# Bias of a top-3 expert layer as one bf16 pass over three-part factors, and a new order of the side work

## The reference

```python
# x: (8, 512, 256)
q, k = rope(x @ Wq.T), rope(x @ Wk.T)            # one head of 256, bf16
o = sum over keys of exp(q k / 16), causal        # one number per token
x = layernorm(x + relu(o * fc1_w + fc1_b) @ fc2_w.T + fc2_b)
xa = x @ P_w.T
C1, C2, C3 = top-3 softmax weights of xa @ U.T over 12 experts, for U1, U2, U3
h = gelu(sum_e C1[:, e] * (x @ W1[e].T))
y = sum_e C2[:, e] * (h @ W2[e].T) + C3 @ b2
out = layernorm(x + y)
```

## Time and profile before

| | us |
|---|---|
| median of 3 runs (323.3 to 323.86) | 323.63 |
| the profiled execution, its own time | 323.53 |
| its span, first to last instruction | 321.8 |
| busy: TensorE / VectorE / ScalarE / POOL | 282.4 / 250.2 / 155.8 / 115.0 |

### The profile page before, as it was taken

One profiled execution on the slowest core, in us unless ns is written; L12 is line 12 of the kernel. 1 busy time (PEld: TensorE's weight loads), 2 busy tenths in 40 slices (PEclk: granted clock), 3 DMA queues, 4 the chain that ended last, 5 costly groups with the idle time before them and its releaser, 6 DMA issues.

```text
span 321.8 us, 6235 instructions
## 1 busy us (share of the span) xinstructions
PE 282.4 (88%) x1976; PEld 191.8 (60%) x1978; DVE 250.2 (78%) x744; ACT 155.8 (48%) x327; POOL 115.0 (36%) x264
## 2 busy tenths in 40 slices
PE   0999999979784989999999999999999997989981
PEld 0444455444333668677677667677678576667770
DVE  0169789999976579689789879888978977887672
ACT  1138747657561381435635634633733753724331
POOL 1000028999999102142332331522333324132221
PEclk9999999999985999999999999999999999999998
DMA  8999999900000000000010001000100010011011
GB/s 232 415 404 229 200 151 211 144 3 0 0 1 0 3 2 0 18 18 18 18 33 17 18 18 29 22 18 18 34 20 16 18 34 19 18 33 26 26 35 37
DMA packets 19235, 20.58 MB, mean 64 GB/s; under 512 B 1600, under 2 KB 18432, under 8 KB 18688
## 3 DMA queue, kind: packets, MB, share of 16 engines
q1 hardware_dynamic: 18480, 19.22, 24.8%
q10 hardware_dynamic: 720, 0.93, 1.0%
HBM read 15.94 MB, written 4.19 MB: 63 GB/s over the span
## 4 chain that ended last, share of the span: by engine, by line
DVE 25%; PE 21%; issue 6%; ACT 5%; POOL 3%; DVEq 0%; POOLq 0%
PE bank L832 17%; DVE early L1202 11%; DVE st L1239 3%; DVE stats L1038 2%; DVE top L1059 2%; ACT x L548 2%; DVE early L1244 2%; PE bank L784 2%; ACT early L657 1%; POOL rstd L391 1%; PE bank L741 1%; DVE mv L1240 1%; ACT x1T L555 1%; ACT early L604 1%; DVE esum L1104 1%
## 5 line engine op out<-in xcount | busy, mean ns | idle before, releaser
L832 PE MATMUL bank<-W,early 128*128 (+1 forms) x630 | 75.5, 273 | 4.4 <-DVE early L1244 2.3
L832 PE MATMUL bank<-W,x1T 128*128 (+1 forms) x630 | 76.9, 277 | 0.5 <-DVE early L1202 0.3
L832 PEld LDWEIGHTS bank<-W,x1T 128*128 128x128 f16 x630 | 60.3, 99 | 19.8 <-DVE early L1202 9.5
L688 PE MATMUL bank<-early,wqk 128*128 128x512 f32 x128 | 64.3, 634 | 8.5 <-DMA gatew<-in_gate 8.5
L1202 DVE SCALAR_TENSOR_TENSOR early<-bank,Csel,early 128x256 f32<-128x256 f32 x124 | 59.3, 479 | 15.0 <-PE bank L832 10.5
L832 PEld LDWEIGHTS bank<-W,early 128*128 128x128 f16 x630 | 60.1, 98 | 14.8 <-DVE early L1244 3.3
L457 POOL TENSOR_SCALAR ve<-mv 128x1 f32<-128x1 f32 x32 | 7.3, 230 | 117.2 <-DVE mv L1240 117.2
L688 PEld LDWEIGHTS bank<-early,wqk 128*128 128x128 f32 x128 | 23.5, 201 | 30.1 <-issue 20.9
L604 ACT ACTIVATE early<-early 128x256 f32<-128x256 f32 x32 | 13.3, 417 | 48.0 <-DVE early L1202 47.9
L499 ACT ACTIVATE qk<-bank 128x512 bf16<-128x512 f32 x32 | 19.0, 594 | 35.6 <-PE bank L688 35.4
L599 ACT ACTIVATE early<-bank,Csel 128x256 f32<-128x256 f32 x31 | 14.6, 472 | 31.0 <-PE bank L832 30.7
(11 more groups left out here) (107 smaller groups left out, 422.3 us busy)
## 6 DMA issues: line engine op xcount, KB each, us to landing
early<-in_xT SPq DMA_DIRECT2D x16, 256.0 KB, 9.8
xs<-in_x SPq DMA_DIRECT2D x32, 128.0 KB, 7.3
out<-early SPq DMA_DIRECT2D x32, 128.0 KB
W<-in_w1T SPq DMA_DIRECT2D x1, 2048.0 KB, 12.0
W<-in_w2T SPq DMA_DIRECT2D x1, 2048.0 KB, 12.3
W<-in_w1T SPq DMA_DIRECT2D x1, 1024.0 KB, 7.6
W<-in_w2T SPq DMA_DIRECT2D x1, 1024.0 KB, 13.8
wqk<-in_wqkT ACTq DMA_DIRECT2D x1, 512.0 KB, 3.8
```

The lines of the kernel that those rows point to most:

```text
L688: mm = pe.matmul(bank[PROJ[n % 2]][:, :], wqk[:, k, g, :], xTb[:, c % 4, k, :, :].rearrange("p s n -> p (s n)"), start=(k == 0), stop=(k = ...
L832: mm = pe.matmul(where[:, 0:DIM], lhs(hx, c), w, start=(k == 0), stop=(k == 5))
```

## The change

The factors of the bias are written as three bf16 parts each (a = a1 + a2 + a3). Of the nine products six are kept; they are laid side by side along the contraction, 6 x 12 = 72 rows, so that one bf16 matmul per tile makes the bias. b2 is split on POOL at the start and spread by six DMAs; C3 is split on POOL in every group, transposed by four bf16 transposes into bank XPOSE and copied by ScalarE. TensorE runs 28 matmuls on zeros at the start, and waits for the constants later. The places of the side work in `aux` change on every engine (`early` almost not at all), and some of the seam between chunks and tiles.

```diff
+LEFT, RIGHT = (0, 0, 0, 1, 1, 2), (0, 1, 2, 0, 1, 0)
+NP = len(LEFT)
-        b2s = sb("b2s", [P, 2 * DIM], F32)
+        b2s = sb("b2s", [NP * NE, DIM], BF16)
-        C3T = sb("C3T", [P, P], F32)
+        C3T = sb("C3T", [NP * NE, GT, P], BF16)
...
+        def routed(g):
+            return 1 <= g < NG
+        def later(g):
+            return 2 <= g < NG
# SP
             load_chunk(1)
+            sp.dma_start(b2f[:, :], b2e[1:NS, :]).then_inc(ld_b2, 16)
...
             sp.dma_start(fc2s[:, :], fc2).then_inc(ld_rows, 16)
-            sp.wait_ge(zero_done, 1)
-            for t in range(GT):
-                sp.dma_start(b2s[rows, ...], b2e[rows, :]).then_inc(ld_rows, 16)
+            sp.wait_ge(b2_split, 1)
+            for k in range(NP):
+                sp.dma_start(b2s[NE * k:NE * (k + 1), :], b2p[:, RIGHT[k], :]).then_inc(b2_spread, 16)
# POOL
+            def C3_split(g):
+                wait(pool, C3T_done, g)
+                f = C3f[:, :, :].unsqueeze(2)
+                link(pool.tensor_copy(C3[:, :, 0:3, :], f.to_broadcast([P, GT, 3, NE])))
+                link(pool.tensor_tensor(C3f[:, :, :], C3f[:, :, :], C3[:, :, 0, :], ALU.subtract))
+                link(pool.tensor_copy(C3[:, :, 3:5, :], f.to_broadcast([P, GT, 2, NE])))
+                pool.tensor_tensor(C3[:, :, 5, :], C3f[:, :, :], C3[:, :, 3, :], ALU.subtract).then_inc(C3_done, 1)
# places in aux (k, s, pos), group in brackets; before -> after
# POOL: norm_scale(k+2) (1,1) -> (0,1); chosen_exps(k+1) (2,1) -> (2,0); weights_of(k+1) (3,1) -> (2,1);
#       C3_split(k+1) new at (3,0); select_of(k+1) (3,1)
# ACT:  C3T_copy(k) (0,0); exp_route(k+1) (1,0) -> (0,0); normed(k+2) (2,0),(2,1) -> (1,1),(2,1);
#       x1_high(k+2, 0) (3,0) -> (2,0); x1_high(k+2, 1): (0,0) of the next k -> (3,1)
# PE:   route_logits(k+1) (0,1) -> (0,0); C3_transpose(k) (0,0); fc(k+2, 1) (0,1);
#       bias(k, 0), bias(k, 1) (1,1),(2,1) -> (0,1),(1,1); x1_transpose(k+2, 0) (2,1) -> (2,0);
#       route_count(k+1) (3,0) -> (2,1); fc(k+3, 0) (3,1) -> (2,1); x1_transpose(k+2, 1) (3,1)
# DVE:  route_max(k+1) (0,1) -> (0,0); fc_add(k+2, 1) (1,0) -> (0,1); route_strike (1,0),(2,0) -> (0,1);
#       norm_stats(k+2) (1,1) -> (0,1); bias_add (2,0),(3,0) -> (1,0),(1,1); route_mask (2,1) -> (1,0);
#       route_sums (3,1) -> (2,0); fc_add(k+3, 0) (0,0) of the next k -> (2,1); route_ids (3,1) -> (2,1);
#       x1_low(k+2, 0) (3,0); x1_low(k+2, 1): (0,0) of the next k -> (3,1)
# PE
             def C3_transpose(g):
                 pe.wait_ge(C3_done, g + 1)
-                pe.wait_ge(ids_done, g + 1)
-                pe.transpose(bank[MISC][:, 0:P], C3[:, :, :].rearrange("p t n -> p (t n)"), identf[:, :])
+                wait(pe, C3T_copied, g)
+                pe.wait_ge(x1lo_done, begun["x1T"])
+                for t in range(GT):
+                    tr = pe.transpose(spread[:, t * P:(t + 1) * P], C3[:, t, :, :].rearrange("p k e -> p (k e)"),
+                                      const(C_IDENT, P))
             def bias(g, h):
                 pe.wait_ge(C3T_copied, g + 1)
+                wait(pe, fc_added, begun["fc"])
+                wait(pe, bias_added, begun["bias"])
-                mm = pe.matmul(bank[ROWS][:, :], C3T[rows, :], b2s[rows, :], start=True, stop=True)
+                for t in (2 * h, 2 * h + 1):
+                    mm = pe.matmul(bank[ROWS][:, t % 2 * DIM:(t % 2 + 1) * DIM], C3T[:, t, :], b2s[:, :], start=True, stop=True)
# PE, start
-            pe.wait_ge(ld_const, 16 * 6)
+            pe.wait_ge(zero_done, 1)
+            for n in range(WARM):            # 28
+                pe.matmul(bank[SCORE[n % 2]][:, 0:DIM], zeros[:, 0:P], zeros[:, :], start=True, stop=True)
             pe.wait_ge(ld_qk, 16)
                 project(c, 1)
                 if c == 0:
+                    pe.wait_ge(ld_const, 16 * 6)
# PE, seam
             x1_transpose(1, 1)
             route_count(0)
-            aux(0, 0, 0)
             first(range(0, 4))
+            fc(2, 0)
             scores(NCH - 1, 0)
             first(range(4, 7))
             scores(NCH - 1, 1)
             first(range(7, NE))
             gate_transpose(NCH - 1)
+            aux(0, 0, 0)
             aux(0, 0, 1)
# ACT: the wait for ld_const moves behind qk_copy(0, 1)
-            aux(0, 0, 0)
-            aux(0, 0, 1)
+            x1_high(1, 1)
             begin(0)
             exps(NCH - 1, 0)
             exps(NCH - 1, 1)
             gate_relu(NCH - 1)
+            aux(0, 0, 0)
+            aux(0, 0, 1)
             gelu(0)
# DVE, seam: in first_mixture, after slot 3 of tile 0
+                    if t == 0 and j == 3:
+                        fc_add(2, 0)
-            aux(0, 0, 0)
+            x1_low(1, 1)
             first_mixture(0)
+            aux(0, 0, 0)
             aux(0, 0, 1)
```

More of the change, by code:

```diff
@@ L166, in build @@
         RING, HT = 4, 4
+        WARM = 28
         Z = GT * NR * NE
@@ L432, in aux @@
             def aux(k, s, pos):
[L433 to L439, removed]
+                if (s, pos) == (0, 1):
+                    if later(k + 2):
+                        norm_scale(k + 2)
+                if (s, pos) == (2, 0):
+                    if routed(k + 1):
+                        chosen_exps(k + 1)
+                if (s, pos) == (2, 1):
+                    if routed(k + 1):
+                        weights_of(k + 1)
+                if (s, pos) == (3, 0):
+                    if routed(k + 1):
+                        C3_split(k + 1)
+                if (s, pos) == (3, 1):
+                    if routed(k + 1):
+                        select_of(k + 1)
             piece = 0
@@ L448, in _ @@
             select_of(0)
+            C3_split(0)
             for i in range(NT + 2):
@@ L577, in aux @@
                 if (s, pos) == (0, 0):
-                    if group(k + 1):
-                        x1_high(k + 1, 1)
                     if group(k):
                         C3T_copy(k)
[L582 to L589, removed]
+                    if routed(k + 1):
+                        exp_route(k + 1)
+                if (s, pos) == (1, 1):
+                    if later(k + 2):
+                        normed(k + 2, 0)
+                if (s, pos) == (2, 0):
+                    if later(k + 2):
+                        x1_high(k + 2, 0)
+                if (s, pos) == (2, 1):
+                    if later(k + 2):
+                        normed(k + 2, 1)
+                if (s, pos) == (3, 1):
+                    if later(k + 2):
+                        x1_high(k + 2, 1)
             def begin(t):
@@ L720, in peak_spread @@
                 pe.matmul(bank[MISC][:, P:P + 3], ones3[:, :], diag[:, :], start=True, stop=True).then_inc(bcast_done, 1)
+            begun = {"fc": 0, "bias": 0, "x1T": 0, "C3T": 0, "logits": 0, "count": 0}
             def fc(g, h):
@@ L738, in x1_transpose @@
                 wait(pe, x1lo_done, 2 * g + h)
+                wait(pe, C3T_copied, begun["C3T"])
+                begun["x1T"] += 1
                 for t in range(2):
@@ L749, in route_logits @@
                     pe.wait_ge(scale_done, 1)
-                wait(pe, C3T_copied, g)
+                wait(pe, ids_done, begun["count"])
+                wait(pe, dz_done, begun["logits"])
+                begun["logits"] += 1
                 for t in range(GT):
@@ L761, in route_count @@
                 pe.wait_ge(mask_done, g + 1)
+                wait(pe, dz_done, begun["logits"])
+                begun["count"] += 1
                 tiles = range(1 if g == 0 else 0, GT)
```

144 lines of the change are left out of this document (79 added, 65 removed).

## The result

The changed kernel takes 313.89 us (median of 4 runs, 312.37 to 317.69) against 323.75 for the kernel before beside it: a ratio of 0.968, 95% interval 0.961 to 0.975. The ratio is of the three fast runs, 312.37, 312.41 and 315.38; those of 317.69 and 318.85 count as slow. The forecast was 308.5 with a range of 303.0 to 315.5, so it was right in sign and range and 5.4 us too hopeful.

What follows compares the result with a forecast made beforehand. In the loop neither TensorE nor VectorE was taken to be at its floor, each waiting for the other. Terms 0 - 0.7 + 2.3 - 11.9 - 4.7 = -15.0 from the profiled 323.53 gave 308.5 us, range 303 to 315.5.

Steps and rivals of the forecast that it cites:

- The bias pass as TensorE's work: Each loop group: bias matmuls 0.48 instead of 2.10 us, transposes 0.24 instead of 0.16; net -1.5 us on TensorE.
- C3_split at 0: POOL, each group: an estimated 1.6 us of splitting costs 0, hidden a tile and a half ahead of its transpose.
- ScalarE's exponentials: Router's exponentials moved to (0, 0): table load 1.28 us, exponential 1.29 after it, done 0.4 before VectorE needs hT; cost 0.
- The loop, -11.9: Five groups go from 25.58 to 23.2 us each: x1T waits go, VectorE's 22.9 plus 0.3 remains; -11.9 in all.
- The prediction's own sign of being wrong: Wrong if groups exceed 24 us, first tiles wait for hT's copy, or rope starts at 11 and stays 3 ahead.
- Rival 3: Loop: TensorE's halt at the bias reaches 2.4 us, the clock falls, groups take 26.5, total 325.0; chance 0.05.
- rival 1: Loop stays coupled: a new wait replaces VectorE's old ones, groups take 23.9 to 24.8, 314.5 at 24.4; chance 0.22.
- The start, 0: Projections' start: earlier TensorE gains nothing overall, as ScalarE's w_sum waits for W2; 0, ends -3.6 and +1.
- my fear: Start: TensorE stands 2.7 us for qk copies, and the clock may fall as behind 2.37; loss up to 1.7.
- Seam, -0.7: Between chunks and tiles: VectorE's first add 3.0 us earlier, cold fc(2, 0) and slot take 2.3 back; -0.7.
- Group 0, +2.3: First tiles: x1_transpose(2, 0) delays the second mixture, +2.9, slow clock behind that halt +1.6, 2.2 saved again; +2.3.
- The last two groups, -4.7: Drain: four bias halves save 3.2 us, logits(7) moved ahead 0.7, idle time 0.8; -4.7, ends -3.2 and -5.8.

Runs made afterwards that it cites:

- experiment 5: The kernel before with the bf16 bias pass in the old order, C3's split left out (all six parts written with the same value): ratio 0.992, about 321.5 us.
- experiment 3: The changed kernel with the old fp32 bias pass and no C3_split, so the new order and warm-up alone: 322.39 us, ratio 0.993.
- experiment 6: The changed kernel with the old fp32 bias pass and bias(k, 0) moved one place later, to (1, 0): 310.97 us, ratio 0.960.
- Experiment 4: The kernel before with the new bias pass alone, C3_split right behind the weights on POOL, old order, no warm-up: 343.97 us, ratio 1.063.
- experiment 1: The changed kernel with 14 matmuls on zeros ahead of every bias(k, 0), filling TensorE's halt: 310.27 us, ratio 0.957.
- Experiment 8: The changed kernel with bias(k, 0) moved to (1, 0) and without the 28 warm-up matmuls: 305.24 us, ratio 0.940 against 0.941 with them.
- experiment 7: The changed kernel with 6 matmuls on zeros ahead of every bias(k, 0): 310.76 us, ratio 0.959.

## Why the prediction was right and wrong

Its terms were 0 - 0.7 + 2.3 - 11.9 - 4.7 = -15.0; measured, by the marks, were -0.4 for the first two, +3.65, -5.7 and -5.9.

- **The bias pass as TensorE's work: right in size.** In the old order (experiment 5) it takes TensorE's busy time from 23.96 to 22.52 per group, 1.4 where I counted 1.5. In the new order TensorE is busy 21.5 instead of my 22.4: there it is 22.97 or 23.35 even with the old pass (experiments 3 and 6), 0.6 to 1.0 less than before, and why the order alone lowers it stays open.
- **C3_split at 0: right, with its condition.** I named the cover, a tile and a half. Experiment 4 shows that without it TensorE stands for 2.03 us where it stood 0.30 before, so 1.7 more (I had said 1.6).
- **ScalarE's exponentials: right.** The load took 1.28 and the exponential started 1.30 after it, in the new place as in the old:

```profile
168.86 1.28 ACT L578 ACT_TABLE_LOAD   x1
...
170.16 0.32 ACT L578 ACTIVATE ez<-dz 128x144 f32<-128x144 f32 x1
```

- **The loop, -11.9: the step that failed.** The prediction says that the new halt is 0.8 us, "TensorE's leftover", and that TensorE "may stand there without starving VectorE". I counted each engine's work per group and took the longer sum. But a wait that ties a TensorE instruction to a VectorE instruction in mid-group closes a path that takes some work from each. It is 23.53 us long, and with the halt of 1.64 (0.40 more ahead of the next mixture) TensorE is the bound again: 21.49 + 1.64 + 0.40 = 23.53. That the halt is no leftover is shown by experiment 3, where 1.5 us more of work left it at 1.7 and made the group 1.2 longer. The path costs 0.3 per group against the forecast's 23.2, and 0.85 against the 22.68 that the kernel reaches without the wait. The prediction's own sign of being wrong, groups above 24, came up in three of the five.
- **The clock: most of the miss in the loop.** The loop took 122.2 us where the forecast had 5 x 23.2 = 116.0, and 116.7 with the clock kept up: 5.5 of the 6.2 are the clock, 0.7 the path. Rival 3 had this mechanism, with the point "from a halt of 2.4 on" taken from the only row I had, at 2.37. It acts at 1.64 in three groups of five, and costs 1.2 us in the first, 2.9 in the fourth and 1.6 in the fifth (24.06 against the 22.46 of experiment 1). These are the figures of the profiled execution, at a mean clock of 0.942; two shorter runs had 0.949. One row at which the clock fell bounds the halt only from above; I used it as a threshold.
- **The number of rival 1** (24.4 per group, 314.5) is what came out (24.4 is the mean), and its words, that a new wait takes the old ones' place, are true too. But most of the way from 23.2 to 24.4 is the clock, which this rival doesn't name, so that the measured time lies within the range is in part luck.
- **The start, 0: right**, with its reason. TensorE projects from 7.34 on, and stands 1.81 us for the copies behind w_sum (I had said 2.7), which waits for W2. The clock stayed up there, against my fear. Experiment 8 shows that the warm-up brings nothing measurable to the total.

```profile
7.34 3.67 PE L733 MATMUL bank<-early,wqk 128*128 128x512 f32 x8 [1.44 <-DMA early<-in_xT]
...
26.19 1.91 ACT L554 ACTIVATE junk<-W 128x2048 bf16<-128x2048 f32 x1 [2.05 <-DMA W<-in_w2T]
...
28.87 1.98 PE L733 MATMUL bank<-early,wqk 128*128 128x512 f32 x4 [1.81 <-ACT qk L537]
```

- **Seam, -0.7: about right** (-0.4 with the start), and fc(2, 0) took 2.07 as said, twice its 1.05.
- **Group 0, +2.3: right in kind, 1.3 too small.** About half of that is a slip of the sum: the last two groups are credited with logits(7), and group 0 isn't charged with logits(2), 0.6 us, which move ahead of its mark in the same way. The rest goes with the clock, which fell earlier than I had it: not behind the transpose's wait (1.11) but behind the 1.34 ahead of bias(0, 0), and it stayed down for some 11 us (the last line below is the window from 116 to 128, at 0.57). So the first tile's mixture ran slow as well, and the next began at 124.82 instead of 122.3.

```profile
116.86 0.51 PE L843 MATMUL bank<-b2s,C3T 72*128 72x256 bf16 x2 [1.34 <-issue]
...
123.91 1.12 PE L792 MATMUL bank<-identf,x 128*128 128x128 f32 x4 [1.11 <-ACT x L586]
...
116.00:128.00 12.00, 9.47 (x47) 6.72 (x48) 7.36 (x29) 4.86 (x9) 2.07 (x5) 0.57 0.01 1
```

- **The last two groups, -4.7: right in kind.** They gave 5.9, a little past the end of -5.8, at a full clock throughout; 0.7 of it is logits(7), moved and not saved.

## What to carry to other kernels

When one instruction of one engine is made to wait for another's in mid-loop, don't only compare the engines' sums. Add up the path that this wait closes: from there through the one engine to where the other takes over, and back to the wait; its length is a lower bound for the iteration. A halt on such a path doesn't shrink when the waiting engine gets more work. Then look for a place one step later at which the wait is already met, which here was worth 9 us for a move of two lines. A standstill of TensorE has a second price, the clock behind it, which falls on the work that follows: if it can't be taken away, matmuls on zeros in a bank nobody reads are worth trying, but not where TensorE is the bound. And two halves of a change can be worth little apart and more together: with the halt in, the order gave 1.6 us alone, the pass 2.6 under the old waits (with its split left out), and both 9.9; without the halt the order gave 13 and the pass 6 on top, as it relieves the engine that the order leaves as the bound.

## What was unexpected in the hardware

The granted clock fell to 0.50 (1.2 GHz) behind halts of 1.64 us in some groups and not in others of the same kernel, and once behind 0.87 (3.59 us for 18 matmuls in experiment 7); yet it stayed at 1.00 behind the 1.81 us at the start. Two windows of the changed kernel, both around the same halt:

```profile
171.00:175.00 4.00, 2.05 (x18) 1.57 (x19) 3.79 (x21) 0.71 (x2) 1.11 (x4) 1.00 0.01 2
...
219.00:223.00 4.00, 3.09 (x14) 1.97 (x15) 2.82 (x17) 0.94 (x2) 1.68 (x4) 0.55 0.02 4
```

The mean clock differs between runs of one kernel, and the time with it: 0.949 in the changed kernel's two of 312.4, 0.942 in the one of 315.38. Only one execution of each kernel was traced, so whether other groups are hit in other runs isn't shown. The Trainium skill (TensorE: Matmul & The Clock Gate, A second HAM failure mode: psum-queue depth-cycling) tells of short idle times between groups of matmuls that make the clock go back and forth; the trace agrees that far. What decides in which group it falls stays open.
